# Router logits: from transposed logits that are copied and turned, to token rows written directly

## The reference

```python
xf = layernorm(x).reshape(-1, 256)          # 2048 token rows
logits = xf @ gate_w.T                      # 2048 x E, E = 8 or 16
probs = softmax(logits)
topk_p, topk_i = top_k(probs, 2)            # two experts per token
y = sum over the two of p * expert_i(xf)    # plus a shared expert
x = x + 0.5 * (y + shared(xf))
```

## Time and profile before

| | |
|---|---|
| median of 3 runs | 3355.32 us (3347.15 to 3362.59) |
| profiled execution, first to last instruction | 3352.4 us |
| PE busy | 2886.6 us, 86% |
| PE weight loads (PEld) busy | 2571.8 us, 77% |
| DVE busy | 2246.5 us, 67% |
| POOL busy | 1704.0 us, 51% |
| ACT busy | 1489.5 us, 44% |
| mean granted clock of PE | 0.918 of full |

### The profile page before, as it was taken

The page is one execution under the profiler, slowest core; times in us unless marked ns, Lnnn a source line. Parts: engine busy times, 40 slices in busy tenths (PEclk is TensorE's granted clock), DMA queues, the critical chain, the costliest instruction groups (busy, mean ns, idle before and its releaser), DMA issues. The chain is left out here.

```text
span 3352.4 us, 60248 instructions
## 1 busy us (share of the span) xinstructions
PE 2886.6 (86%) x21018; PEld 2571.8 (77%) x21018; DVE 2246.5 (67%) x5794; ACT 1489.5 (44%) x3235; POOL 1704.0 (51%) x1645
## 2 busy tenths in 40 slices
PE   8979999999999898876897968479996858976898
PEld 6869999999999787865686957367775847965687
DVE  6767777777777667755536666568886545655655
ACT  3255666666656424335323443344444334433342
POOL 2355556565656317444406356458886546340743
PEclk9989999999999899997898968779998869988899
DMA  2022221212121202230103434400002443330333
GB/s 72 1 74 70 54 70 54 71 54 70 54 70 54 69 1 82 75 103 27 37 0 98 125 99 118 114 18 2 2 2 70 125 119 85 114 99 0 95 103 97
DMA packets 129187, 221.68 MB, mean 66 GB/s; under 512 B 18609, under 2 KB 68145, under 8 KB 128881
## 3 DMA queue, kind: packets, MB, share of 16 engines
q1 hardware_dynamic: 95026, 147.47, 14.8%
q0 software_dynamic: 21216, 57.96, 6.7%
q10 hardware_dynamic: 12672, 12.58, 1.1%
HBM read 170.23 MB, written 47.72 MB: 65 GB/s over the span
## 5 line engine op out<-in xcount | busy, mean ns | idle before, releaser
L1632 POOL DMA_INDIRECT MXG<-dxn,IDX x250 | 237.3, 949 | 231.9 <-PE bank L1204 171.9
L1642 POOL DMA_INDIRECT YG<-dyo,POSI x192 | 187.3, 976 | 215.7 <-DMA dyo<-YS 112.5
L2519 POOL TENSOR_SCALAR SX<-SX,MN 128x256 f32<-128x256 f32 x256 | 233.7, 928 | 57.2 <-DVE MN L2443 57.1
L1615 POOL TENSOR_TENSOR MWL<-RAW,MWH 128x608 fp32r<-128x608 f32 (+2 forms) x118 | 181.2, 1543 | 43.2 <-ACT MWH L1307 37.0
L2443 DVE CUSTOM_DVE_ANT_0 SX<-bank,FMASK 128x128 f32<-128x128 f32 (+1 forms) x512 | 156.1, 351 | 51.5 <-PE bank L2333 51.4
L1026 POOL TENSOR_TENSOR HL<-HID,HH 128x512 fp32r<-128x512 f32 x56 | 72.4, 1294 | 223.9 <-ACT HH L993 223.4
L515 PE MATMUL bank<-MWH,GH 128*128 x500 | 173.8, 348 | 10.1 <-DVE HB L1555 4.7
L515 PE MATMUL bank<-MWH,SHH 128*128 128x256 f32 x352 | 111.7, 317 | 73.2 <-POOL SHL L1486 29.2
L1329 ACT ACTIVATE GH<-bank 128x256 fp32r<-128x256 f32 x250 | 96.7, 387 | 173.5 <-PE bank L1204 161.2
L1613 POOL CAST MWH<-RAW 128x608 fp32r<-128x608 f32 (+2 forms) x78 | 56.8, 728 | 220.6 <-DVE X L901 120.7
L517 PE MATMUL bank<-MWH,GL 128*128 x500 | 157.8, 316 | 0.0
(11 more groups left out here) (459 smaller groups left out, 11615.3 us busy)
## 6 DMA issues: line engine op xcount, KB each, us to landing
dyo<-YS SPq DMA_DIRECT2D x250, 128.0 KB
RAW<-in_wheads SPq DMA_DIRECT2D x68, 320.0 KB
RAW<-in_eL SPq DMA_DIRECT2D x64, 304.0 KB
BB<-dgates SPq DMA_DIRECT2D x68, 256.0 KB, 3.6
GB<-dgates SPq DMA_DIRECT2D x68, 256.0 KB, 4.3
dxn<-XN ACTq DMA_DIRECT2D x16, 512.0 KB
RAW<-in_eL SPq DMA_DIRECT2D x32, 256.0 KB
RAW<-in_sL SPq DMA_DIRECT2D x18, 384.0 KB
```

Source lines behind the costliest of these rows:

```text
L1615: nc.gpsimd.tensor_tensor(MWL[:, at_:at_ + cols], RAW[:, n % RAW_SLOTS, 0:cols], f32(MWH[:, at_:at_ + cols]), ALU.subtract).then_inc(w_rea ...
L1632: nc.gpsimd.indirect_dma_start(MXG[:, n % XGS, :], None, dxn, bass.IndirectOffsetOnAxis(ap=IDX[:, b:b + 1], axis=0)).then_inc(x_in[n % XGS ...
L1642: nc.gpsimd.indirect_dma_start(YG[:, i % YGS, :], None, dyo[0:m.blocks * P, :], bass.IndirectOffsetOnAxis(ap=POSI[:, c * NT + t:c * NT + t ...
L2519: nc.gpsimd.tensor_scalar(part, part, MN[:, n % RING2, 1:2], None, ALU.subtract).then_inc(s_less1, 1)
```

## The change

The logits are computed directly as token rows. For each tile of a pair and each half k of the 256 features, the 128 x 128 block of XTH (or XTL) is the stationary operand and 16 router columns move, in the usual three products (`mm3`), accumulated into the 16 columns of bank 4 that the sum wrote before. A pair takes 12 matmuls. The copy on ACT, the turning sum on PE, the semaphores `logits` and `lg_sb`, the tiles LGS and HALVES and the zero columns of RWS go away, and the loops over the front are one iteration shorter.

```diff
         def front_tensor(pe, st):
             pe.wait_ge(consts, 4)
-            for g in range(GROUPS + 2):
+            for g in range(GROUPS + 1):
...
-                if st.routed:
-                    if g >= 2:
-                        logits_sum(pe, st, 2 * g - 4)
-                        logits_sum(pe, st, 2 * g - 3)
-                    if 1 <= g < GROUPS + 1:
-                        moe_logits(pe, st, 2 * g - 2)
-                        moe_logits(pe, st, 2 * g - 1)
+                if st.routed and g:
+                    moe_logits(pe, st, 2 * g - 2)
+                    moe_logits(pe, st, 2 * g - 1)
...
         def moe_logits(pe, st, p):
 
             pe.wait_ge(xt_lo, st.tr * HALF + p + 1)
-            if p >= 2:
-                pe.wait_ge(lg_sb, HALF * st.rt + p - 1)
-            o = bank[p % 2][0:32, 0:2 * P]
-            for k in range(KC):
-                x = slice(p * 2 * P, (p + 1) * 2 * P)
-                nc.tensor.matmul(o, RWS[:, st.router, k, 0:32], XTH[:, k, x], start=k == 0, stop=False)
-                last = nc.tensor.matmul(o, RWS[:, st.router, k, 32:64], XTL[:, k, x], start=False, stop=k == KC - 1)
-            last.then_inc(logits, 1)
-
-        def logits_sum(pe, st, p):
-
-            pe.wait_ge(lg_sb, HALF * st.rt + p + 1)
-            for q in range(2):
-                t = 2 * p + q
-                last = nc.tensor.matmul(bank[LOGIT][:, t * 16:(t + 1) * 16], LGS[:, p % 2, q * P:(q + 1) * P], HALVES[:, :],
-                                        start=True, stop=True)
+            for t in (2 * p, 2 * p + 1):
+                o = bank[LOGIT][:, t * 16:(t + 1) * 16]
+                for k in range(KC):
+                    last = mm3(o, xt(k, t * P, P), (RWS[:, st.router, k, 0:16], RWS[:, st.router, k, 16:32]), k == 0, k == KC - 1)
             last.then_inc(r_logits, 1)
-
-        def logits_high(act, st, p):
-
-            act.wait_ge(logits, HALF * st.rt + p + 1)
-            if p >= 2:
-                act.wait_ge(r_logits, HALF * st.rt + p - 1)
-            nc.scalar.activation(LGS[:, p % 2, :], bank[p % 2][0:32, 0:2 * P], ACT.Copy).then_inc(lg_sb, 1)
...
                         if k == done + 3:
                             moe_logits(pe, nx, 2 * g)
                             moe_logits(pe, nx, 2 * g + 1)
-                        if k == done + 4:
-                            logits_sum(pe, nx, 2 * g)
-                            logits_sum(pe, nx, 2 * g + 1)
...
-                    if k == done + 3 and nx.kind == 'moe':
-                        logits_high(act, nx, 2 * g)
-                        logits_high(act, nx, 2 * g + 1)
```

## The result

The changed kernel took 3397.31 us (median of 5 runs, 3382.23 to 3399.53), the kernel before 3355.32 on the same chip. The ratio is 1.0118, with a 95% interval from 1.0101 to 1.0135: slower by 1.2%. 3399 was forecast, in a range of 3364 to 3416. The profiled execution of after was the fastest of its runs, with a span of 3380.0 us against 3352.4 before, so the two traces differ by 27.6 us where the medians differ by 42.

A forecast was written before the change was run, and what follows sets the result against it. PE's issue was taken to bound the fronts: 39.6 us for six fronts plus 3.2 and 1.5 for the tails made 44.3, a span of 3396.7 and a forecast of 3399 us, range 3364 to 3416.

The forecast's parts named there:

- What bounds the kernel: All eight routed stages wait for the last logits, and what PE issues bounds the front; waits grow some 6 us a stage.
- 0.110 us a load: In the new logits matmuls, each 128-column load sets 0.110 us from start to start at full clock, 0.213 at the lower.
- The rival of a faster stream: Loads with short products in the fronts follow each other at 0.06 us, giving 3338 us; 5% chance.
- Issue, +2.3 a front: In each one-piece front at full clock: group 0 +1.6, next group +0.7, end no change; 13.8 us in six.
- The clock, +4.3 a front: PE's low clock twice within each one-piece front: +2.5 us in the last stream, +1.8 over a turning and warm burst.
- the rival in which the clock holds: PE keeps full clock in the fronts, so only issue costs stay: 18.5 us, 3374 us; 20% chance.
- The rival of still more low clock: Two middle groups and the shared matmuls behind are slow too, 9 to 10 us more a front, 3415 to 3425; 8% chance.
- The tails: In the two tails, at the low clock, logits end later: +3.2 us into moe:L2 and +1.5 into moe:L3.
- All of the delay goes through to the end: Behind the fronts and tails, gathers wait for the routing chain's end, so the full 44.3 us reaches the end.
- absorption: Behind the fronts, a later wait for POOL's weight pieces or gathers takes up the delay, 3360 to 3367 us; 7% chance.

The follow-up runs named there:

- third: The changed kernel with only the product of the high parts, 4 matmuls a pair in place of 12; 3331.57 us, 0.9950 of before.
- pair: The changed kernel with 256-column products, warm behind the first group only, and two loads a product for three; 3277.25 us, 0.9960 of before.
- experiment 2: The changed kernel with each logits product moving 256 columns, the 16 router columns sixteen times over, same loads; 3365.95 us, 1.0065 of before.
- experiment 5: The kernel before with 56 more warm matmuls ahead of the last logits of the six one-piece fronts; 3373.22 us, 1.0077 of before.

## Why the prediction was right, point by point

- **What bounds the kernel.** Right. The first routing steps waited for PE in all eight stages, 17.1 us longer in all, and the kernels whose fronts were clearly shorter (third, pair) were faster. The waits grew by 2.1 us a stage and not by some 6, because DVE was itself later, as I had allowed for: in the first front its last XTL ended 3.2 us later into the front.
- **0.110 us a load.** Right, 0.112: over the group that starts at 20.88, 24 starts in 2.68 us. Of the 768 matmuls, 467 started 0.11 us after the one ahead and 260 started 0.21 after it. The rival of a faster stream falls with this. (I called the 107 ns of the Trainium skill, page "TensorE: Matmul & The Clock Gate", section "LDWEIGHTS (loading the stationary operand)", a measurement; what stands there is a formula, the columns over 1.2 GHz. These starts are 5 ns above it.)
- **Issue, +2.3 a front.** About right. The second turning came at 23.56 (23.6 forecast). The smallest fronts are +3.9 to +4.6 with one low stretch in each; taking off half of the low time that each has over before (3.4 to 4.7 us) leaves 2.2 to 2.3.
- **The clock, +4.3 a front.** Right in kind, and experiment 2 shows it by itself: the rival in which the clock holds is out. The mean clock is 0.914, under the 0.918 of before, as forecast. In the six fronts the low time went from 15.2 to 59.2 us; at half speed 22 of the 44 are lost, 3.7 a front. The rival of still more low clock did not come either: no front was over +7.9. The size is right only as a mean: it comes as 4 to 5 or 7 to 8 us, by how many low stretches a front catches. The place varies as well: the first front lost it in turning and `warm` and had 1.00 in its last stream, the second lost it over two bursts of `warm` and again in its last stream.
- **The tails.** 4.1 for 4.7 forecast: +3.4 into moe:L2, +0.7 into moe:L3 (3.2 and 1.5 forecast). The wait at the end of both grew by 1.6 us, from 3.04 to 4.68, where I had 1.5. The whole of a tail moves by more than that between two traces, as the table shows, so the agreement of the sum proves little.
- **All of the delay goes through to the end.** This step failed. I had given absorption 7%, as an alternative to the forecast, and with POOL's pieces named only for the tail into moe:L3. It is a part of every outcome: 12 us of 39 in the traces of before and after, 10 of 36 in the medians of experiment 5. I had looked for what else would be waited for, and not for what would run faster when it ran later: beside less of POOL's work DVE's steps between the first routing step and IDX took 134.8 us in four stages for 143.4 before, and these stretches came out 5.7 us shorter. The traced run, at 3380.0, is 16.7 us under the 3396.7 worked out for a span: 12 of these are the give-back, and 5 the fronts (39.3 for 44.3). The forecast met the median all the same, because that trace was the fastest of its runs, 15 us under the median; what made the others longer no trace shows. That the median, 3397, came within 2 us of the 3399 forecast owes something to luck; on the second chip the ratio was 1.0100, which would be 3389.

Open stays the rest of the give-back: 9.4 us in the four attention stages of the changed kernel, but 1.7 in the delayed one, and 2.6 lost in the changed kernel's second trace. No experiment was aimed at it, and the two traces of the changed kernel differ by more than its size there.

## What to carry to other kernels

Where the load of the stationary operand sets the pace, count loads, not columns: a narrow product costs nearly as much as a wide one at the full clock, and twice as much when it loses the clock. Filling such products with columns that nobody reads was cheaper here, and can be elsewhere, than bursts of idle matmuls in between. And before a delay or a gain on a critical path is carried to the end one for one, look at which engine works beside the steps that follow it: the same steps ran in 0.42 us or in 0.92, by whether POOL was done.

## What the runs showed of the hardware

- PE lost the clock in streams without a gap, when each load of 128 columns was followed by a product of 16 (0.50 in 1159.0 to 1162.2). With 256 columns behind the same loads it kept it better: 14.7 us low in the six one-piece fronts, where the narrow products had 59.2 and 68.0 in their two traces and the kernel before 15.2.
- A load of 128 columns sets 0.112 us from start to start with products of 16 columns, and 0.121 with products of 256; at the lower clock 0.213 with 16.
- DVE operations with two SBUF inputs of 256 columns took 0.42 us alone, 0.61 to 0.74 beside POOL subtractions of 192 columns, and 0.71 to 0.92 beside POOL's pieces of 512 (the steps L1384 and L1385 of the second moe:L2); a scalar_tensor_tensor, with two such inputs as well, 1.49 for 0.42. The reductions, with one input, kept 0.42.
